# Attention and expert kernel on one core: projections run three pairs ahead instead of two

## The reference, cut to what matters

```
xl = layer_norm(x, local gains);  xg = layer_norm(x, global gains)
q, k, v = x* @ wq.T + bq, x* @ wk.T + bk, x* @ wv.T + bv      (x* is xl or xg; 16 heads of width 8)
local = softmax(q k') v @ wo.T + bo    on xl, positions 0..31 of each batch
glb   = softmax(q k') v @ wo.T + bo    on xg, all 256 positions of each batch
x     = layernorm(x + local + glb)
tokens -> 8 experts, top 1 by x @ Wg, at most 1024 tokens for each, in order of the tokens
out   = layernorm(x + gate * (relu(x @ W1[e] + b1[e]) @ W2[e] + b2[e]))    (no expert for tokens beyond 1024)
```

## Time and profile before

| what | us |
|---|---|
| median of 3 runs (lowest, highest) | 724.46 (724.17, 726.23) |
| the profiled execution: its time | 722.03 |
| its span, first to last instruction | 720.2 |
| busy: PE, DVE, ACT, POOL | 635.0, 559.0, 494.3, 470.1 |
| PE weight loads, beside the matmuls | 358.3 |

### The profile page before, as it was taken

How to read it: one execution, slowest core, us unless ns; L and a number is a source line. 1 busy time by engine, 2 the same in 40 slices (tenths; PEclk the granted TensorE clock), 3 DMA queues, 4 the chain that set the end, 5 groups by cost and what they waited for, 6 DMA issues and landing times.

```text
span 720.2 us, 19327 instructions
## 1 busy us (share of the span) xinstructions
PE 635.0 (88%) x6502; PEld 358.3 (50%) x6502; DVE 559.0 (78%) x1722; ACT 494.3 (69%) x1131; POOL 470.1 (65%) x957
## 2 busy tenths in 40 slices
PE   3569698997999999999999999999999349999993
PEld 2335354443455454544554545445444227767673
DVE  6647598995999999899999988998894205676775
ACT  2327477894988888889888888898888334354431
POOL 4513244657788888888888888886676712554546
PEclk9659899998999999999999999999999769999997
DMA  5693668955467776494685664845721122433321
GB/s 123 162 205 119 131 176 210 233 193 113 128 127 188 203 146 160 105 202 134 125 189 139 143 162 106 183 134 108 189 49 35 31 67 61 114 101 102 96 84 39
DMA packets 144177, 95.73 MB, mean 133 GB/s; under 512 B 12100, under 2 KB 139933, under 8 KB 144080
## 3 DMA queue, kind: packets, MB, share of 16 engines
q1 hardware_dynamic: 138944, 85.82, 49.9%
q0 software_dynamic: 4096, 7.81, 3.5%
q10 hardware_dynamic: 1040, 0.87, 0.4%
HBM read 47.70 MB, written 45.74 MB: 130 GB/s over the span
## 4 chain that ended last, share of the span: by engine, by line
PE 55%; DVE 21%; issue 7%; DMA 6%; SPq 5%; POOL 3%; ACT 2%; POOLq 0%; ACTq 0%; DVEq 0%
DVE mx L1034 12%; PE ps_o L614 11%; PE ps_b L587 8%; PE ps_a L1480 7%; PE ps_a L569 4%; PE ps_b L1474 4%; PE ps_m L645 2%; PE ps_f L528 2%; PE ps_m L660 2%; PE ps_f L523 2%; PE ps_f L518 2%; SPq L351 2%; PE ps_a L1474 2%; PE ps_f L1474 2%; PE ps_m L639 2%
## 5 line engine op out<-in xcount | busy, mean ns | idle before, releaser
L1034 DVE TENSOR_REDUCE mx<-ps_a 128x2 f32<-128x512 f32 (+1 forms) x576 | 359.7, 650 | 60.1 <-PE ps_a L569 58.3
L838 ACT ACTIVATE prob<-ps_b 128x512 f32<-128x512 f32 (+1 forms) x576 | 298.9, 572 | 74.5 <-PE ps_b L587 73.3
L587 PE MATMUL ps_b<-qs,ks 59*128 59x256 bf16 (+1 forms) x1152 | 190.6, 271 | 12.8 <-DMA qs<-mT 5.6
L569 PE MATMUL ps_a<-ks,qs 56*128 56x256 bf16 (+1 forms) x1152 | 188.6, 274 | 13.4 <-DMA ks<-stack 11.2
L614 PE MATMUL ps_o<-prob,vp 128*32 128x256 f32 (+1 forms) x2304 | 172.0, 383 | 0.4 <-ACT prob L838 0.4
L587 PEld LDWEIGHTS ps_b<-qs,ks 59*128 59x128 bf16 x1152 | 80.7, 95 | 103.9 <-ACT prob L838 50.4
L1624 POOL DMA_INDIRECT out<-res,dest x64 | 62.3, 973 | 75.8 <-DVE res L1597 60.7
L1324 POOL DMA_INDIRECT routed<-row,slot x64 | 67.2, 1050 | 35.1 <-issue 25.9
L569 PEld LDWEIGHTS ps_a<-ks,qs 56*128 56x128 bf16 x1152 | 75.9, 96 | 25.6 <-DMA ks<-stack 12.0
L614 PEld LDWEIGHTS ps_o<-prob,vp 128*32 128x32 f32 x2304 | 49.7, 109 | 57.9 <-issue 49.7
L1480 PE MATMUL ps_a<-w_sb,prob 128*128 128x128 f32 x512 | 61.4, 280 | 2.1 <-ACT prob L1532 2.1
(11 more groups left out here) (153 smaller groups left out, 1039.8 us busy)
## 6 DMA issues: line engine op xcount, KB each, us to landing
stack<-part SPq DMA_DIRECT2D x36, 384.0 KB, 3.9
qs<-stack SPq DMA_DIRECT2D x72, 192.0 KB
ks<-stack SPq DMA_DIRECT2D x72, 192.0 KB
stack<-part SPq DMA_DIRECT2D x36, 256.0 KB, 3.8
stack<-part SPq DMA_DIRECT2D x36, 128.0 KB, 3.8
routed<-empty SPq DMA_DIRECT2D x8, 520.0 KB, 6.2
rows_sb<-routed SPq DMA_DIRECT2D x16, 260.0 KB, 3.8
xt<-x SPq DMA_DIRECT2D x16, 256.0 KB
```

The costliest lines, as they stand in the source:

```text
L569: ins = nc.tensor.matmul(ps_a[:, n % 3, qt * S:qt * S + keys.stop - keys.start], qs[half, b, hp, qt * P:(qt + 1) * P], ks[half, b, hp, key ...
L587: ins = nc.tensor.matmul(ps_b[:, 1 - e, kt * n:(kt + 1) * n], ks[half, u % STACKS, hp, kt * P:(kt + 1) * P], qs[half, u % STACKS, hp, quer ...
L838: nc.scalar.activation(prob[:, hp, half * n:(half + 1) * n], ps_b[:, half, 0:n], ACT.Exp).then_inc(exp_done, 1)
L1034: nc.vector.reduce_max(mx[:, u % 2, :, col], ps_a[:, n % 3].rearrange("p (t k) -> p t k", t=2)[:, :, 0:k], axis=AX).then_inc(max_done, 1)
```

## The change

AHEAD becomes 3 for the steps, and a new constant OPEN = 2 keeps the old number for the two pairs that use the prologue's own PSUM banks. Pair 2 moves from steps 0 and 1 into the prologue, between the ten first groups of maxima, and uses ps_f as every later pair does. Every pair p from 3 on is now projected in steps 2(p - 3) and 2(p - 3) + 1, two steps sooner. The ring vp grows from 6 to 8 buffers. On SP, a unit is loaded in every step, at its start, three units ahead; stores stand in step 0 (units 4 and 5) and at the end of odd steps (u + 5 and u + 6), so that at least a step lies between a store and its load. Clears run in steps 1 to 6, and pair 4's x is loaded in the prologue. The weights of expert 0 are loaded in step 12 and those of expert 1 in step 15, instead of both in step 12.

```diff
-AHEAD = 2
+AHEAD = 3
+OPEN = 2
+VBUF = 8
...
         def step(u):
             p = first_pair(u)
             if there(u):
                 place_max(u, 1)
-            if u % 2 == 0 and 2 < u + 2 < U:
-                load_stack(u + 2)
-            if u == 0:
-                load_stack(3)
+            if u + 3 < U:
+                load_stack(u + 3)
...
                 place_max(u + 1, 0)
-            if u % 2 == 0 and 3 < u + 3 < U:
-                load_stack(u + 3)
             if p is not None and p + 2 < NPAIR:
                 load_x(p + 2)
-            if u % 2 == 1 and u + 3 < U:
-                store_stack(u + 3)
-                store_stack(u + 4)
-            if LU - 1 <= u < LU + 4:
-                clear_routed(2 * (u - LU) + 1 if u > LU - 1 else 0)
-            if LU <= u < LU + 3:
-                clear_routed(2 * (u - LU) + 2)
-            if u == LU + 8:
-                tail.first_weights(sp)
+            if u == 0:
+                store_stack(4)
+                store_stack(5)
+            if u % 2 == 1 and u + 5 < U:
+                store_stack(u + 5)
+                store_stack(u + 6)
+            if 1 <= u < 7:
+                clear_routed(u - 1)
+            if LU <= u < LU + 2:
+                clear_routed(u + 2)
+            if u in (LU + 8, LU + 11):
+                tail.first_weights(sp, (u - LU - 8) // 3)
...
+        load_x(4)
         place_max(0, 0)
...
             if n == 1:
                 turn_bv()
+                turn_x(OPEN, 0)
+                turn_x(OPEN, 1)
             if n == 3:
                 project_bv()
+                project_in(OPEN, "q", 0)
+                project_in(OPEN, "q", 1)
+            if n == 7:
+                project_in(OPEN, "k", 0)
+                project_in(OPEN, "k", 1)
...
+        project_in(OPEN, "v", 0)
+        project_in(OPEN, "v", 1)
...
         copy_bv()
+        scale_shift(OPEN)
+        first_part_q(OPEN)
         copy_max(0, 0)
+        first_part_k(OPEN)
+        second_part(OPEN)
+        place_v(OPEN, 0)
+        place_v(OPEN, 1)
...
-            late = first + 1 if first is not None and AHEAD + 1 < first + 1 < NPAIR else None
+            late = first + 1 if first is not None and first + 1 < NPAIR else None
...
-                    input_stats(late, (2, 3))
+                    input_stats(late, (2, 3) if late > AHEAD + 1 else (0, 1, 2, 3))
...
+            if n == 6:
+                take_rest_q(OPEN)
+            if n == 9:
+                take_rest_k(OPEN)
...
         split_max(0, 0)
         split_max(0, 1)
+        third_part(OPEN)
```

47 lines of the change are left out of this document (23 added, 24 removed).

## The result

| | before | changed |
|---|---|---|
| median on the same chip (lowest, highest), us | 725.35 (724.17, 726.85), 4 runs | 717.96 (716.99, 719.45), 4 runs |
| the profiled execution, us; its span | 722.03; 720.2 | 717.12; 715.3 |

The ratio is 0.9909, with a 95% interval of 0.9885 to 0.9934: the change makes the kernel faster by 0.91% or 7.4 us. I had forecast 12.5 us. So the direction and the range held, and the size was little more than half of what I expected. The two profiled executions lie 4.9 us apart, so an account of these two profiles has 4.9 us to explain.

The account below looks back on a forecast made before the run. PE is busy nearly throughout the middle, so gains lie at the attention's two ends. Terms -7.7 - 2.8 - 6.9 + 1.2 + 3.7 = -12.5 us take 724.46 us to 712.0 us; range 705 to 720 us.

Parts of the forecast that it names:

- The scatter's wait: Step 8: clears issued by the end of step 6 end POOL's 5.76 us wait at the first scatter; gain 7.7 us.
- One pair fewer: Steps 30 and 31: pairs end at step 29, so these two have none; gain 2.8 us.
- Unit 4's load: Step 2: the load, issued in step 1, no longer stalls PE for 4.44 us; gain 6.9 us.
- SP's queue in steps 0 to 3: Local steps: SP's longer list makes mT rows late in steps 1 to 3; loss 3.7 us.
- The prologue: Before step 0: pair 2's added work, 4.86 us on PE, mostly fits PE's wait; loss 1.2 us.
- Edits at nothing: Moved loads of the first experts' weights, and middle loads no longer right behind their stores, change nothing.
- (a): Local steps run free: stores issue faster, TensorE's clock is up by step 0; -17.4 us, 707 us; chance 0.20.
- (b): Steps 0 to 3: transfers collide, landings are slow, unit 4's load waits 4 us for stores; 718.5 us; chance 0.18.
- (c): Step 7: POOL stands for something else that the clears covered, so 7.7 us stay; 719.7 us; chance 0.06.
- (d): Odd steps 5 to 29: loads ahead of mT rows cost 1.6 us each, so slower, 732.8 us; chance 0.06.

Follow-up runs that it names:

- e1: The kernel before with only its eight clears moved, two in each of steps 3 to 6; ratio 0.9951 to the kernel before.
- the changed kernel's third profile: The changed kernel, unchanged, run once more on another chip; ratio 0.9891 to the kernel before.
- e6: The changed kernel with the mask-row transfers of units 4 to 7 issued by ACT instead of SP; ratio 0.9823 to the kernel before.
- e5: The changed kernel with mT rows for the next step issued ahead of the residual's x and y's store in steps 0 to 3; ratio 0.9848 to before.
- e11: The changed kernel with mask rows of units 4 to 7 cleared by ACT's transfers and both first experts' weights in step 12; ratio 0.9872 to before.
- e13: On top of e11, ACT lays pair 2's v out behind the first exponentials instead of before them; ratio 0.9828 to the kernel before.
- e14: The same kernel as e11, run a second time on another chip; ratio 0.9802 to the kernel before.

## Why the prediction was right in direction and wrong in size

**The scatter's wait: right.** Forecast -7.7 us, measured -7.9 us, and e1 shows that the clears' places alone do it. This rested on a wait of 5.76 us and on the whole undisturbed step as the measure, not on the wait alone; the step gave more than the wait, as forecast.

**One pair fewer: right.** Forecast -2.8 us, measured -2.4 us in steps 28 to 34.

**Unit 4's load: right, though step 2 alone doesn't look it.** Step 2 took 14.08 us where this term has 11.8 us. But 1.76 us of it are a wait for mT rows, which the forecast charges to SP's queue, so the term missed by 0.5 us: 12.3 us at a granted clock of 0.86. In the changed kernel's third profile step 2 without its wait took 11.6 us at 0.92. The clock is also why the step gave more than the wait of 4.44 us: before, it ran at 0.82. Step 1 of before was a quiet step, with the DMA engines busy for 0.29 of it, but that did no harm to it as a measure of PE's work: in e6 it took 12.30 us at a DMA share of 0.88, 9.9 us without its wait of 2.40 us.

**SP's queue in steps 0 to 3: the step that failed.** The mechanism held and the term was mis-sized. Forecast +3.7 us over the 33.6 us that steps 1 to 3 would otherwise last; measured 42.45 us, so +8.9 us on the same base. The waits for mT rows are 7.7 us of these, and 1.2 us are PE's work at a clock of 0.96, 0.86 and 0.85 where 1.00 was taken. Two things in the working went wrong.

- The landing. I took the quick one of 1.91 us, and it comes from a stretch in which the DMA engines were busy for 0.17 of the time. The rows of the change cross stretches at 0.63 to 0.92 and landed after 2.94 to 3.82 us. The chain of before had 3.98 us in step 0, at 1.10, and the worst of the earlier trace rows, 4.96 us, was at 1.03; either was the nearer row.
- The end of the sum. I followed SP's list to the rows that open step 3 and stopped. Up to there the waits are 5.2 us, within my own 3.2 to 6.3 us. The rows that open step 4 cost another 2.4 us, by the load, the residuals and y that step 3 itself puts ahead of them.

e5 and e6 show that the place in the list is one cause, and the landings of e6, e11, e13 and e14 that it isn't the only one. e6 comes to 50.4 us to step 4 where the forecast has 98.0 - 46.48 - 1.2 = 50.3 us; that is a coincidence, since the forecast counts the mask rows in SP's list.

**The prologue: mis-sized.** Forecast +1.2 us, measured +2.4 us (and +2.0 us between the repeats of before and of the change on one chip, 47.86 and 49.85 us). I took pair 2 for 4.86 us of PE. The changed kernel's timeline, PE, has its four parts, transposes, q, k and v:

```profile
33.66 1.06 PE L502 MATMUL ps_f<-ident,xh 128*128 128x128 f32 x4
...
36.91 1.91 PE L525 MATMUL ps_f<-xg,wqkv_sb 128*128 128x256 f32 x4
...
42.19 1.50 PE L530 MATMUL ps_f<-xg,wqkv_sb 128*128 128x256 f32 x4
...
45.62 2.05 PE L520 MATMUL ps_f<-wqkv_sb,xg 128*128 128x128 f32 x8 [0.69 <-DVE rest L1023]
```

That is 6.52 us, 1.66 us more. The row from which I took q says x2; it was half of a q, since project_in runs once for each half. A look at the count beside the duration would have shown it, and q and k together came to 1.0 us more than forecast. The other 0.7 us is v: its row began at 25.84 us, and the clock before was full for more than half of that row (0.50 up to 26.4 us), while the new v ran at 0.50.

**Edits at nothing: the weights were not.** I named the time until the experts start as cover, and did not ask what stands behind these loads in SP's list, nor who waits for that: steps 16 and 17 are 1.6 us longer. Another 1.4 us of the gain were lost after step 35 had opened, where the first up-projection (four matmuls) took 3.53 us instead of 2.94 us; the cause of that is open.

**The rivals.** (a) is refuted: no version ran the local steps free. With the fuller prologue step 0 ran at a granted clock of 0.69, 0.60 and 0.55 in the three profiles of the changed kernel and lasted 12.12, 12.74 and 13.56 us, where before it ran at 0.59 and lasted 13.04 us (13.18 us in the repeat). The Trainium skill (TensorE: Matmul & The Clock Gate, section What's actually happening) let one expect a sooner release of the clock from more activity; one profile of three shows it. (b) came out in half. Its sign, step 4 opening after 102 us, was met (103.44 us), and landings were slow, if not at the slowest; but the 4 us that unit 4's load was to wait for its stores didn't come. That the median, 717.96 us, lies next to its 718.5 us is partly luck: other terms, the prologue and the weights among them, fill the place of those 4 us. (c) is refuted by the scatter's row. (d) is refuted: steps 8 and 9 of the changed kernel last 14.83 + 13.69 us, and step pairs further on 28.77 us as before.

**Where the gain went.** Of -12.5 us, 10.3 us came from the scatter and the pair. The 3.2 us expected in steps 1 to 3 turned into +2.0 us, 5.2 us worse: 4.0 us because PE waited 7.7 us for mT rows and not 3.7 us, and 1.2 us by PE's work at a lower clock. The prologue, the weights and the experts' start cost 4.1 us more than forecast; steps 0 and 4 to 7 gave 1.8 us that I had not counted.

## What to carry to other kernels

Where a change crowds a stage, take the price of a landing from a row in which the DMA engines are as busy as they will be, and look up how busy they were beside each row that you take. Follow a queue to the end of the stage, not to the first place where it runs late. Put a wait into one term only, and check each term against the step without the other terms' waits. Ahead of small transfers that an engine waits for at each step's opening, every issue counts. Handing two bulk transfers a step to ACT helped the stage here; handing it four stalled the engine that computes for the one that waits. Read the count beside a duration before multiplying it.
